# An attention layer over a sorted edge list: the last 32 tiles' logits and segment maxima in two halves

## What is computed

```python
h = relu(layernorm(x)) @ W_node.T                 # [12500, 4, 32]
e = edge_attr_64 @ W_edge.T                       # [212500, 4, 32]
att = sum(concat([h[src], h[dst], e], -1) * a, -1)
att = where(att > 0, att, 0.2 * att)
m = maximum(segment_max(att, dst), 0.0)
ex = exp(att - m[dst])
denom = segment_sum(ex, dst) + (N_EDGES - deg)[:, None] * exp(-m)
out = x + segment_sum((ex / denom[dst])[:, :, None] * h[src], dst)
```

## Time and profile before

| | |
|---|---|
| median of 3 runs | 2218.95 us (2217.8 to 2221.28) |
| the profiled execution, its time | 2223.87 us |
| its span, first to last instruction | 2221.9 us |
| PE / PEld busy | 1396.4 us (63%) / 1248.5 us (56%) |
| DVE busy | 1605.7 us (72%) |
| ACT busy | 913.3 us (41%) |
| POOL busy | 1618.3 us (73%) |
| mean granted TensorE clock | 0.644 of full speed |

### The profile page before, as it was taken

One profiled execution on the slowest core, in us unless ns is written; L12 is line 12 of the kernel. 1 busy time (PEld: TensorE's weight loads), 2 busy tenths in 40 slices (PEclk: granted clock), 3 DMA queues, 4 the chain that ended last, 5 costly groups with the idle time before them and its releaser, 6 DMA issues.

```text
span 2221.9 us, 39684 instructions
## 1 busy us (share of the span) xinstructions
PE 1396.4 (63%) x9479; PEld 1248.5 (56%) x9480; DVE 1605.7 (72%) x4606; ACT 913.3 (41%) x2653; POOL 1618.3 (73%) x1689
## 2 busy tenths in 40 slices
PE   6366566656665666566666666666656666666665
PEld 5255555655655556556555555565555556555654
DVE  7667777777676777776777777767777777677777
ACT  4134434444344344443444434434434344344344
POOL 4577777777777777777777777777777777777770
PEclk9665666666666666666566566665566655766566
DMA  7933333333333333333333333333333333333320
GB/s 220 309 99 105 88 106 88 89 106 88 90 106 85 105 89 88 105 89 89 103 88 106 89 88 106 88 95 97 87 106 88 88 106 88 88 104 88 106 69 24
DMA packets 120203, 224.80 MB, mean 101 GB/s; under 512 B 40693, under 2 KB 80501, under 8 KB 113413
## 3 DMA queue, kind: packets, MB, share of 16 engines
q0 software_dynamic: 53440, 114.07, 21.8%
q1 hardware_dynamic: 65565, 110.07, 15.2%
q10 hardware_dynamic: 1168, 0.35, 0.1%
HBM read 180.37 MB, written 43.98 MB: 101 GB/s over the span
## 4 chain that ended last, share of the span: by engine, by line
POOL 36%; issue 22%; DVE 15%; PE 15%; DMA 5%; DVEq 4%; ACT 3%; ACTq 0%; POOLq 0%; SPq 0%
POOL gath L442 36%; DMA gath<-h_table,idx 4%; PE bank_w L1183 4%; PE bank_z L1125 4%; DVE onehot_b L669 4%; PE bank_t L1150 3%; PE bank_rn L1133 2%; DVE held L833 2%; DVE vals L775 2%; DVEq L77 1%; ACT held L1001 1%; PE bank_rn L1143 1%; DVE s_sum L731 1%; DVE out_buf L840 1%; DVE lk L750 1%
## 5 line engine op out<-in xcount | busy, mean ns | idle before, releaser
L442 POOL DMA_INDIRECT gath<-h_table,idx x1661 | 1591.1, 958 | 519.7 <-issue 503.5
L1150 PE MATMUL bank_t<-ident_b,onehot_b 128*128 128x128 bf16 x1672 | 175.8, 269 | 407.5 <-DVE onehot_b L669 407.5
L1183 PE MATMUL bank_p<-vals,onehot 128*128 128x137 f32 x1664 | 401.4, 433 | 0.7
L1150 PEld LDWEIGHTS bank_t<-ident_b,onehot_b 128*128 128x128 bf16 x1672 | 129.7, 121 | 457.6 <-DVE onehot_b L669 457.6
L1183 PEld LDWEIGHTS bank_p<-vals,onehot 128*128 128x128 f32 x1664 | 375.4, 326 | 5.9 <-issue 0.2
L1183 PE MATMUL bank_w<-vals,onehot 128*128 128x137 f32 x1664 | 361.8, 400 | 0.0
L1183 PEld LDWEIGHTS bank_w<-vals,onehot 128*128 128x128 f32 x1664 | 336.1, 295 | 17.4 <-DVE vals L775 17.2
L1031 ACT COPY onehot_t<-bank_t 128x1024 bf16<-128x1024 bf16 x209 | 211.5, 1012 | 309.2 <-PE bank_t L1150 307.8
L669 DVE SCALAR_TENSOR_TENSOR onehot_b<-bank_w,base,zz 128x1024 bf16 (+1 forms) x209 | 268.3, 1284 | 20.4 <-ACT zz L948 1.2
L1160 PE MATMUL bank_s<-s_live,onehot_t 128*128 128x24 bf16 x1672 | 75.7, 179 | 249.3 <-ACT onehot_t L1031 249.3
L1125 PEld LDWEIGHTS bank_z<-w_edge_bd,ef 128*128 128x128 f32 x1664 | 219.9, 216 | 7.1 <-DMA ef<-in_edges 7.1
(11 more groups left out here) (164 smaller groups left out, 1984.2 us busy)
## 6 DMA issues: line engine op xcount, KB each, us to landing
ef<-in_edges SPq DMA_DIRECT2D x52, 1024.0 KB
out_x<-out_buf SPq DMA_DIRECT2D x210, 128.0 KB
gath<-h_table,idx POOLq DMA_INDIRECT x1661
h_table<-gath SPq DMA_DIRECT2D x14, 462.0 KB, 4.5
x_all<-in_x SPq DMA_DIRECT2D x14, 448.0 KB, 10.0
out_x<-x_all SPq DMA_DIRECT2D x14, 448.0 KB, 11.9
resets<-ef SPq DMA_DIRECT2D x8, 416.0 KB
flag_rows<-resets SPq DMA_DIRECT2D x52, 64.0 KB
```

Of the source, the lines that this page charges most:

```text
L442: e.indirect_dma_start(gath[:, q * GPS + g, t * ROW:(t + 1) * ROW], None, table, bass.IndirectOffsetOnAxis(idx[:, q, g * TILES + t:g * TIL ...
L1150: ins = e.transpose(bank_t[:, :].bitcast(BF16)[:, t * P:(t + 1) * P], onehot_b[buf][:, t, :], ident_b[:, :])
L1183: ins = e.matmul(half_p[q], onehot[q][:, t, :], vals[q][:, t, :], start=(t == 0), stop=(t == TILES - 1))
```

## The change

The z stage of super 51 is done in two halves of 16 and 13 gathered tiles, that is groups 0 and 1, then groups 2 and 3.

- POOL's gathers of groups 0 and 1 of super 51 count up a new semaphore `d_half`; those of groups 2 and 3 count up `d_gath` as before. The gathers themselves and their order stay.
- SP raises `gathered` for super 51 once the first 16 have landed, at the same place as before (beside the second step of pair 101), and once more for the rest beside the second step of pair 102 (`rest_landed`).
- The first half's z stage stands where the whole one stood. Its `z_columns`, `z_copies` and `z_maxima` handle 2 groups. The transposes and the scans keep their shapes: all 16 rows, of which 8 are used.
- The second half's z stage is new work, beside the second step of pair 102, on DVE, PE and ACT. It too has the whole transposes and scans.
- `bounds` has one more entry. A new function `half_walk` runs one pair, with a loop for more that doesn't run here. DVE's loop over supers ends one super earlier; super 50 with its stage, pair 102 and pair 103 are written out behind it. The releases of ring places at the ends of the last supers' halves fall away, since nothing waits for them.

```diff
-LAST_LANDED = (GPS - 1) * TILES + LAST_TILES
+HALF = GPS // 2
+LAST_LANDED = (HALF - 1) * TILES + LAST_TILES
...
+def half_walk(nc, e, bounds, b, pair, beside=((None, None),) * 2, pairs=None):
+
+    lo, hi = pairs or load(nc, e, bounds[0:1, bass.ds(b, 2)], [PAIRS - 1, PAIRS])
+    pair(lo, beside)
+    second = e.snap(lo + 1, min_val=1, max_val=PAIRS)
+    with e.If(second < hi):
+        with e.Fori(second, hi) as u:
             pair(u)
     return hi
...
-                n = LAST_LANDED if last_turn and q == RING - 1 else GPS * TILES
-                e.wait_ge(d_gath[q], i * (GPS * TILES * 16) + n * 16)
+                if last_turn and q == RING - 1:
+                    e.wait_ge(d_half, HALF * TILES * 16)
+                else:
+                    e.wait_ge(d_gath[q], i * (GPS * TILES * 16) + GPS * TILES * 16)
                 e.sem_inc(gathered, 1)
...
+            def rest_landed():
+                i, q = SUPERS // RING - 1, RING - 1
+                e.wait_ge(d_gath[q], i * (GPS * TILES * 16) + LAST_LANDED * 16)
+                e.sem_inc(gathered, 1)
...
+            half_walk(nc, e, bounds, SUPERS - 1, pair, (None, rest_landed))
             u_end = nc.s_assert_within(
-                walk(nc, e, bounds, SUPERS - 1, pair, (None,) * 4), 0, PAIRS - 1,
+                half_walk(nc, e, bounds, SUPERS, pair, (None, None)), 0, PAIRS - 1,
...
-            ).then_inc(d_gath[q], 16)
+            ).then_inc(landing, 16)
...
-            chain(e.tensor_copy(bounds[:, 1:SUPERS + 1], ends[0:1, GPS - 1::GPS]))
...
+            chain(e.tensor_copy(bounds[:, 1:SUPERS], ends[0:1, GPS - 1:GROUPS - 1:GPS]))
+            chain(e.tensor_copy(bounds[:, SUPERS:SUPERS + 2], ends[0:1, GROUPS - 1 - HALF::HALF]))
...
-                e.tensor_tensor(zc, z_edge, s1, ALU.add).then_inc(z_cols_done, 1)
+                e.tensor_tensor(zc[:, first:first + n, :, :], z_edge[:, first:first + n, :, :], s1,
+                                ALU.add).then_inc(z_cols_done, 1)
...
-            with e.Fori(1, SUPERS) as b:
+            with e.Fori(1, SUPERS - 1) as b:
                 wait(e, z_ready, b * 4)
                 steps(beside(b, e.snap((b % RING) * GPS, min_val=0, max_val=SLOTS - GPS)))
+            slot0 = (SUPERS - 1) % RING * GPS
+            wait(e, z_ready, (SUPERS - 1) * 4)
+            steps(beside(SUPERS - 1, slot0, HALF))
             wait(e, z_ready, SUPERS * 4)
-            drain(steps(((None, None),) * 4))
+            half_steps(((None, lambda: load_end(SUPERS)),
+                        (lambda: z_columns(SUPERS, slot0, HALF, GPS - HALF),
+                         lambda: scans(SUPERS))))
+            e.wait_ge(z_ready, SUPERS * 4 + 3)
+            drain(half_steps(((None, None),) * 2))
...
-            drain(walk(nc, e, bounds, SUPERS - 1, pair))
+
+            def rest_of_z():
+                z_copies(SUPERS, (SUPERS - 1) % RING * GPS, HALF, GPS - HALF)
+                z_maxima(SUPERS, (SUPERS - 1) % RING * GPS, HALF, GPS - HALF)
+
+            half_walk(nc, e, bounds, SUPERS - 1, pair, ((None, None), (rest_of_z, None)))
+            drain(half_walk(nc, e, bounds, SUPERS, pair))
...
-            walk(nc, e, bounds, SUPERS - 1, pair, ((None, None, None),) * 4)
+            half_walk(nc, e, bounds, SUPERS - 1, pair,
+                      ((None, None, None),
+                       (None, lambda: turn_z(SUPERS), lambda: maxima(SUPERS))))
+            half_walk(nc, e, bounds, SUPERS, pair, ((None, None, None),) * 2)
```

More of the change, by code:

```diff
@@ L156, in build @@
         first_rec = sb("first_rec", [1, 2], I32)
-        bounds = sb("bounds", [1, SUPERS + 1], I32)
+        bounds = sb("bounds", [1, SUPERS + 2], I32)
         ident = sb("ident", [P, P])
@@ L439, in gathers @@
                             settle(e)
-                        last = last_turn and q == RING - 1 and g == GPS - 1
-                        for t in range(LAST_TILES if last else TILES):
+                        last = last_turn and q == RING - 1
+                        landing = d_half if last and g < HALF else d_gath[q]
+                        for t in range(LAST_TILES if last and g == GPS - 1 else TILES):
                             e.indirect_dma_start(
@@ L642, in _, with z_columns @@
             e.sem_inc(n_const, 1)
-            def z_columns(b, slot0):
+            def z_columns(b, slot0, first=0, n=GPS):
                 wait(e, gathered, b + 1)
-                wait(e, e_mm, b * PAIR + PAIR)
-                s1 = gath[:, bass.ds(slot0, GPS), :].rearrange("p g (t c) -> p g t c", c=ROW)[
-                    :, :, :, DIM:ROW]
+                if b is not SUPERS:
+                    wait(e, e_mm, b * PAIR + PAIR)
+                s1 = gath[:, bass.ds(slot0 + first, n), :].rearrange(
+                    "p g (t c) -> p g t c", c=ROW)[:, :, :, DIM:ROW]
                 zc = z_cols[:, :, :].rearrange("p t (g h) -> p g t h", h=HEADS)
-                e.tensor_tensor(zc, z_edge, s1, ALU.add).then_inc(z_cols_done, 1)
+                e.tensor_tensor(zc[:, first:first + n, :, :], z_edge[:, first:first + n, :, :], s1,
+                                ALU.add).then_inc(z_cols_done, 1)
             def scans(b):
-                e.wait_ge(d_reset, b * 16 + 16)
+                if b is not SUPERS:
+                    e.wait_ge(d_reset, b * 16 + 16)
                 wait(e, r_full, b + 1)
@@ L660, in scans @@
                 wait(e, scan_f, b + 1)
-                wait(e, z_ready, b * 4 + 3)
+                wait(e, z_ready, b * 4 + (1 if b is SUPERS else 3))
                 e.tensor_tensor_scan(z_rows[:, ::-1], flag_rows[:, 1, ::-1], rows[:, ::-1], NEG,
@@ L866, in _, with beside @@
             scans(0)
-            def beside(b, slot0):
+            def beside(b, slot0, n=GPS):
                 def step_2():
@@ L873, in beside, with half_steps @@
                 return ((None, None), (None, None), (None, step_2),
-                        (lambda: z_columns(b, slot0), lambda: scans(b)))
+                        (lambda: z_columns(b, slot0, 0, n), lambda: scans(b)))
+            def half_steps(beside):
+                lo = e.snap(first_pair, min_val=0, max_val=PAIRS - 1)
+                hi = e.snap(end_pair, min_val=0, max_val=PAIRS)
+                half_walk(nc, e, bounds, None, pair, beside, (lo, hi))
+                e.reg_mov(first_pair, end_pair)
+                e.reg_mov(end_pair, next_end)
+                return hi
             load_end(0)
```

33 lines of the change are left out of this document (19 added, 14 removed).

## The result

The changed kernel takes 2226.72 us (median of 6 runs, 2225.62 to 2228.09); the kernel before took 2218.68 us in its 6 (2217.13 to 2221.28). The ratio is 1.0032 with a 95% interval of 1.0021 to 1.0043: slower, by 4.7 to 9.5 us. The profiled execution took 2227.83 us, its span is 2226.0 us.

A forecast was written before the change was run, and what follows sets the result against it. POOL's gathers set the pace until the last lands, then a bare DVE, PE and ACT chain. Minus 0.8 us for the wait plus 6.3 us for the second stage gave +5.5 us, 2224.4 us, range 2220.5 to 2227.8 us.

The forecast's parts named there:

- What bounds the kernel: Over most of the run POOL's gathers set the pace; after the last gather a DVE, PE and ACT chain, from 2171.94 us.
- The wait, a gain of 0.8 us: At super 51's z_columns DVE's 1.20 us wait for gathers goes; 0.8 us reaches the end, bounds 0.6 and 1.20 us.
- The second stage, 6.3 us: Beside pair 102's second step the added z stage lies bare on the path: 6.3 us, bounds 6.1 and 6.8 us.
- Half a stage costs as much as a whole one: In the z stage's scans, two groups leave 8 of 16 rows in use but all 1024 columns, and as many transposes.
- What costs nothing: The prologue's bounds copy (0.19 us) and extra register loads are hidden; loads between pairs 102 and 103 uncovered cost under 1 us.
- The sum, +5.5 us: For the whole kernel, minus 0.8 plus 6.3 us, bounds +4.9 and +6.2 us, giving 2224.4 us, 0.25% slower.
- likeliest case: For the whole time, the forecast widened for clock shifts in pairs 102 and 103: +3.9 to +7.2 us, 2222.8 to 2226.2 us; 59%.
- Hidden in part: In pairs 102 and 103, idle gaps and a better clock absorb 1.5 us of the added stage: 2220 to 2223.3 us; 28%.
- Faster: At the last gathers the ordinary wait exceeds about 6.7 us, so splitting pays; at 12 us, 5 us faster, 2214 us; 5%.
- Slower still: Around the added stage, scan waits for transposes and uncovered loads add 1 to 3 us: 2226.5 to 2228 us; 8%.
- The change doesn't do what it says: At the first half's stage DVE still waits, say for a late SP: +6.3 us, 2225.3 us; counted inside the forecast.
- The signs: In the trace, wrong if pair 103 starts before 2201, s_sum follows pair 102's copy within 6 us, or earlier times move over 0.1%.

The follow-up runs named there:

- both halves waiting: Changed kernel with SP raising the first half only when all 29 gathers have landed; ratio 1.0001 (0.9968 to 1.0034) to the kernel before.
- written-out kernel: Kernel before with only DVE's loop over supers ending one earlier and super 50 written out behind it; ratio 1.0004 (0.9986 to 1.0021).
- one stage: Changed kernel without the second half's z stage, DVE only waiting for the remaining gathers; ratio 0.9967 (0.9934 to 0.9999) to the kernel before.
- second stage early: Changed kernel with the second half's z stage beside the first step of pair 102; ratio 0.9998 (0.9966 to 1.0031) to the kernel before.
- short scans: Changed kernel with the second half's two scans over 512 columns of 1024; ratio 1.0017 (0.9987 to 1.0048) to the kernel before.
- eight rows: Changed kernel with the scans of both halves over 8 rows in place of 16; ratio 1.0031 (1.0019 to 1.0043) to the kernel before.
- late gathers in halves: Changed kernel with 12 more gathers ahead of group 2 of super 51; 2241.37 us, ratio 1.0026 (1.0016 to 1.0036) to the kernel before.
- two last experiments: Changed kernel unaltered, 1.0014 (0.9997 to 1.003), and kernel before with only DVE's loop written out, 1.0004 (0.9986 to 1.0021), both against the kernel before.

## Why the prediction held

**What bounds the kernel** stood: POOL's gathers up to the end of the gathers, and then a bare chain in which everything added is paid.

**The wait, a gain of 0.8 us.** The window that has lost it is 0.99 us shorter, in the bounds of 0.6 and 1.20 us, but the reason for 0.8 us didn't hold. The prediction took 5.66 us from `onehot_b` to the last copy as the floor, since `bank_t` had taken 1.04 us. In after it took 0.62 us, and the stretch is 2173.08 - 2167.83 = 5.25 us, 1.23 us less than the 6.48 us of before: the whole wait reached the last copy. Behind the copy 0.25 us were lost again (6.42 us for 6.17 us), since the transposes back took 1.00 us and not 0.65 us. That these two came to nearly what was forecast is luck of the clock.

What the prediction didn't say either is that the wait is no constant. With both halves waiting DVE had no idle time, and in the written-out kernel it had none either, though there the last gather had been issued 37 us before its `s_sum`, on the chip with the long steps. How long a whole stage would have waited in the other executions can be estimated from the 3.75 us of before. DVE came to `z_columns` 3.39 us after the last issue in after (2169.03 - 2165.64), 2.86 us with one stage, 2.87 us with the second stage early, 3.76 us with short scans and 3.80 us with eight rows: a wait of 0 to 0.9 us, 0.4 us of it in after. The tail bears this out. With one stage and no wait it is 53.13 and 53.8 us, 0.8 and 0.15 us under that of before. Against an execution in which DVE comes late by itself the change gains nothing at all.

**The second stage, 6.3 us.** The step with it is 6.75 us longer than before, in the bounds of 6.1 to 6.8 us. Of this 0.42 us stand ahead of the last copy (5.66 us for 5.24 us), as much as `bank_t` took longer in that step (1.04 us for 0.62 us). The scan waited for no transposes; it began 0.07 us after the copy. The part from the last copy on came to 6.33 us more (6.40 - 0.07) where 6.10 were summed: the transposes back took 1.00 us and not 0.65. The prediction's own split of the 6.10 us doesn't add up, since 2.40, 2.27, 0.65 and 0.27 us leave 0.5 us for the handing over and not 0.8 us; the total was read from the whole stretch and isn't touched by it. The tails with two stages are 59.67, 59.45, 59.27, 59.38 and 59.58 us (late gathers in halves among them), those with one stage and no idle time 53.13 and 53.8 us. Mean against mean it is 59.47 - 53.47 = 6.0 us, so 6.75 us has some 0.7 us in it that go with the lower level of the clock in this one execution (0.42 us in `bank_t`, 0.35 us in the transposes back). The tails of either kind spread by 0.4 and 0.7 us.

**Half a stage costs as much as a whole one.** Shown from both sides, by the scans over 8 rows (no change) and over 512 columns (half the time).
**What costs nothing** cost next to nothing. The tail with one stage has the loads without their cover, and 0.19 us show, where under 1 us was said. The copy for `bounds` in the prologue stayed hidden: DVE still waits 11.82 us before the first `z_columns`.

**The sum, +5.5 us.** The tail measured +5.7 us. The whole time measured +7.1 us by the ratio, with an interval from 4.7 us, and +8.0 us between the medians. The other ratios of kernels with both stages in place are 1.0031, 1.0026, 1.0014 and 1.0001, that is 6.9, 5.8, 4.4 and 0.2 us, the last with an interval of 7 us to either side. All of these hold 5.7 us in their intervals, and none shows that something is lost ahead of the tail; that the 2.3 us between 8.0 and 5.7 us are lost there isn't excluded, since the two last experiments, meant to decide it, were too unsteady. The predicted 2224.4 us lies 2.3 us under the measured median, which is in the whole range but 0.5 us above the likeliest case's own, 2222.8 to 2226.2 us. The sum is borne out by the tail; how the whole time came to stand above it stays open.

**The rivals.** *Hidden in part* didn't come: DVE's idle time inside the steps took up none of the scans. The stage one step earlier shows what could have been hidden, 1.6 us, by a place that the change didn't choose. *Faster* has its condition shown: a wait of 16 us turns the sign. *Slower still* asked for 1 to 3 us of waits in the second stage. The median of 2226.72 us lies at the lower end of its 2226.5 to 2228 us, but its mechanism isn't in the trace: the scan waited for nothing, the loads stayed under their cover, and `s_sum` came 0.27 us after ACT's copy had ended. *The change doesn't do what it says* fell with the first half's `z_cols`, which waited for nothing.

**The signs.** By the clock of the trace pair 103 starts at 2200.99, just before the 2201 that was named as a sign of being wrong. That line was drawn from a second `s_sum` of pair 101 at 2167.95, and here it comes at 2166.33, 0.07% earlier and within the tenth of a per cent allowed. Counted from it pair 102 starts after 13.17 us and pair 103 after 34.66 us, where 13.35 and 34.35 us were forecast. The second step of pair 102 takes 13.56 us for the 13.1 us forecast, the next `s_sum` comes 6.40 us after its last copy, over the 6 us named, and from pair 103 to the end it is 25.0 us.

## What to carry to other kernels

Before a stage is split so that its first part needn't wait, compare the idle time that the wait really ends in with the price of the stage's second execution; if the parts are halves along the rows of a scan and not along its columns, that price is the whole stage again. Read the idle time at the one place that is split, not from the mean over the run: it was 3.7 us in the mean and 0 to 1.2 us there (the values between are estimates). If a second stage must be, put it one step ahead of where it is needed, so that PE's and ACT's part of it lies beside DVE's next step; that took 1.6 us off the 6 us here. And where a difference of a few tenths is to be explained, look first at what granted clock PE's pieces had on either side.

## What the runs showed of the hardware that wasn't expected

A scan of two tensors takes 2.28 us for 1024 columns and 1.21 us for 512 on 16 rows, and 2.27 us for 1024 columns on 8 rows. The product `vals` over as many columns and all 128 rows takes 1.22 us, about half. The eight transposes back take 0.64 or 0.65 us at a granted clock of 1.00 and 1.00 us at 0.50, and `bank_t`'s 0.62 and 1.04 us, so that one step of the same program differs by 0.4 us from one execution to the next. And on one chip the same program took 3112 us, with idle times of 4 to 7 us a step ahead of `s_sum` whose releaser the profile names only as remote, as long as gathers were running; from the last gather on its steps were as fast as elsewhere. What held them there stays open.
